# Query weights times keys made once instead of queries for every batch, one more tile weighed by GpSimd, and a new order

## The reference

```python
q = (x @ Wq).reshape(b, t, H, 2, DK)
q1, q2 = (q[..., 0, :], q[..., 1, :])
sim1 = jnp.einsum('bthd,hkd->bthk', q1, keys[:, :, 0, :])
sim2 = jnp.einsum('bthd,hkd->bthk', q2, keys[:, :, 1, :])
s1, i1 = jax.lax.top_k(sim1, K)
s2, i2 = jax.lax.top_k(sim2, K)
all_scores = (s1[..., :, None] + s2[..., None, :]).reshape(b, t, H, K * K)
all_indices = (i1[..., :, None] * NK + i2[..., None, :]).reshape(b, t, H, K * K)
final_scores, pk_idx = jax.lax.top_k(all_scores, K)
final_indices = jnp.take_along_axis(all_indices, pk_idx, axis=-1)
w_down = e_down[final_indices]
w_up = e_up[final_indices]
hidden = jnp.einsum('btd,bthkd->bthk', x, w_down)
hidden = jax.nn.silu(hidden)
hidden = hidden * jax.nn.relu(final_scores)
out = jnp.einsum('bthk,bthkd->btd', hidden, w_up)
```

## Time and profile before

| | us |
|---|---|
| median of three runs | 388.55 |
| profiled execution | 388.38 |
| its span, first to last instruction | 386.5 |

### The profile page before, as it was taken

One profiled execution on the slowest core, in us unless ns is written; L12 is line 12 of the kernel. 1 busy time (PEld: TensorE's weight loads), 2 busy tenths in 40 slices (PEclk: granted clock), 3 DMA queues, 4 the chain that ended last, 5 costly groups with the idle time before them and its releaser, 6 DMA issues.

```text
span 386.5 us, 8279 instructions
## 1 busy us (share of the span) xinstructions
PE 340.7 (88%) x3222; PEld 249.5 (65%) x3222; DVE 333.8 (86%) x838; ACT 246.8 (64%) x371; POOL 140.2 (36%) x194
## 2 busy tenths in 40 slices
PE   2898796688889889999969889998999999989997
PEld 2455453243334337688948767887888887778886
DVE  3989999999989997368877999999999999999940
ACT  3899999999998992237456687755766654011000
POOL 8737524612665644211001104255424148601000
PEclk9999999999989999999998999999999999999999
DMA  8940000000000008000000000000000000000000
GB/s 252 358 137 3 1 0 0 2 0 2 2 0 0 2 1 270 2 0 3 0 2 0 3 0 3 0 3 2 2 17 16 2 15 4 2 15 2 17 15 27
DMA packets 11142, 11.40 MB, mean 29 GB/s; under 512 B 608, under 2 KB 10592, under 8 KB 11104
## 3 DMA queue, kind: packets, MB, share of 16 engines
q1 hardware_dynamic: 11104, 10.88, 8.7%
HBM read 9.83 MB, written 1.05 MB: 28 GB/s over the span
## 4 chain that ended last, share of the span: by engine, by line
DVE 46%; PE 31%; ACT 11%; issue 7%; DMA 2%; POOL 1%; SPq 1%; DVEq 0%; ACTq 0%; POOLq 0%
PE pair L934 7%; DVE arena L1663 6%; PE pair L772 5%; DVE arena L1653 4%; PE pair L626 3%; DVE i L1982 3%; DVE arena L2042 3%; PE pair L898 3%; DVE s L1976 3%; ACT arena L1200 2%; ACT arena L1203 2%; DVE arena L2038 2%; DVE XN L1588 2%; DMA arena<-in_L_ffn_keys_dram 2%; PE pair L920 2%
## 5 line engine op out<-in xcount | busy, mean ns | idle before, releaser
L1663 DVE TENSOR_REDUCE arena<-arena 128x16 f32<-128x1024 f32 x64 | 66.5, 1075 | 2.5 <-POOL arena L365 1.7
L898 PE MATMUL pair<-arena,EDT 128*128 128x256 f32 x256 | 60.2, 383 | 0.0
L934 PE MATMUL pair<-EU,arena 128*128 128x256 f32 x256 | 58.4, 382 | 0.6 <-DVE arena L2066 0.6
L934 PEld LDWEIGHTS pair<-EU,arena 128*128 128x128 f32 x256 | 47.9, 190 | 7.4 <-issue 1.0
L898 PEld LDWEIGHTS pair<-arena,EDT 128*128 128x128 f32 x256 | 47.1, 190 | 6.5 <-ACT arena L1454 0.2
L644 PE MATMUL pair<-arena,WQ 128*128 128x512 fp8e4 x112 | 33.8, 383 | 15.8 <-ACT arena L1203 7.8
L488 POOL TENSOR_TENSOR arena<-arena 128x512 f32<-128x512 f32 x20 | 27.6, 1394 | 45.1 <-ACT arena L1446 45.1
L1200 ACT ACTIVATE arena<-pair,sq_bias 128x1024 f32<-128x1024 f32 x32 | 38.4, 1199 | 2.0 <-issue 1.5
L1186 ACT ACTIVATE arena<-arena,clip_bias 128x1024 fp8e4<-128x1024 f32 x32 | 39.5, 1235 | 0.0
L656 PE MATMUL pair<-arena 128*128 128x512 fp8e4 x128 | 38.6, 384 | 1.0 <-ACT arena L1186 1.0
L1454 ACT ACTIVATE arena<-pair 128x512 f32<-128x512 f32 x32 | 19.0, 598 | 27.2 <-PE pair L898 27.1
(11 more groups left out here) (201 smaller groups left out, 666.1 us busy)
## 6 DMA issues: line engine op xcount, KB each, us to landing
arena<-in_L_ffn_e_down_dram SPq DMA_DIRECT2D x1, 2048.0 KB, 12.5
EU<-in_L_ffn_e_up_dram SPq DMA_DIRECT2D x1, 2048.0 KB, 9.2
arena<-in_L_ffn_w_fc_dram SPq DMA_DIRECT2D x2, 512.0 KB, 5.4
X<-in_x_dram SPq DMA_DIRECT2D x1, 1024.0 KB, 6.2
arena<-in_L_ffn_w_proj_dram SPq DMA_DIRECT2D x1, 1024.0 KB, 13.7
GUW<-in_fside_BxS2xS_dram SPq DMA_DIRECT2D x1, 1024.0 KB, 11.4
out_dram<-arena SPq DMA_DIRECT2D x8, 128.0 KB, 1.7
CTX<-in_ctx_dram SPq DMA_DIRECT2D x1, 512.0 KB, 4.9
```

Source lines behind the costliest of these rows:

```text
L898: last = pe.matmul(bk2(4 + i % 2)[:, r, :], EDT[:, k, at:at + P], xT4[:, b % 2, k, :], start=(k == 0), stop=(k == 1))
L934: last = pe.matmul(bk2(7)[:, n, :], PR[:, n, e, :], EU[:, e, :], start=(e == 0), stop=(e == EROWS - 1))
L1663: dve.tensor_reduce(err[:, g // NS % 2, :, g % NS], squares, AX.X, ALU.add).then_inc(s["reduced"], 1)
```

## The change

1. No queries. The product of query weights and keys is made once: query_weights_transposed() transposes Wq by heads, key_weights(k) multiplies it by the keys, 256 features in two halves k, and ACT copies the result to WK. sims(b, n) multiplies the tokens by WK: four products of 128x512 over 128 rows, where it were eight of 128x128 over 64. WK takes the place of qT4, the transposed weights that of yo, eqs and sums.
2. Tile 5's coefficients are copied by ACT and weighed by POOL; DVE weighs tiles 6 and 7 only.
3. experts(b, ...) waits for the tokens and no longer for the queries' copies.
4. The lists of all engines from ffn1(8) on are in a new order: batch 1's integer layer stands beside batch 0's, ffn2 of batches 0 and 1 comes first, x3(1) and c_round(2) come before top8(0), and the ups and scatters are spread differently.

```diff
-        qT4 = cut(22 * KI, 2 * KI).rearrange("p (s h t) -> p s h t", s=2, h=H)
+        WK = cut(22 * KI, 2 * KI).rearrange("p (k a n) -> p k a n", k=2, a=2)
+        WQT = cut(24 * KI, KI).rearrange("p (h d) -> p h d", h=H)
-        DVE_WEIGHS = NT - 3
+        DVE_WEIGHS = NT - 2
...
-            def half_queries(b, lo, hi_):
-
-                pe.wait_ge(s["d_xT_e"], b + 1)
-                for i in range(lo, hi_):
-                    if b:
-                        pe.wait_ge(s["d_g_e"], 8 * b - 1 + i)
-                    for h in range(2):
-                        for k in range(2):
-                            c0 = (2 * i + h) * P
-                            last = pe.matmul(bk2(4 + i)[:, h, :], WQ1[:, k, c0:c0 + P], xT4[:, b % 2, k, :],
-                                             start=(k == 0), stop=(k == 1))
-                    last.then_inc(s["d_q_t"], 1)
+            def query_weights_transposed():
+
+                pe.wait_ge(ld["wq1"], 16)
+                pe.wait_ge(s["wT_e"], 8)
+                pe.wait_ge(s["guwT_e"], B)
+                for h in range(H):
+                    for k in range(2):
+                        last = pe.transpose(bk2(h // 2)[:, h % 2, k * P:k * P + P], WQ1[:, k, h * P:h * P + P],
+                                            ident[:, :])
+                last.then_inc(s["wqT_t"], 1)
+
+            def key_weights(k):
+
+                pe.wait_ge(s["wqT_e"], 2)
+                if k:
+                    pe.wait_ge(s["wk_e"], 2 * k)
+                for h in range(H):
+                    for a in range(2):
+                        rows = slice(a * DK, a * DK + DK)
+                        last = pe.matmul(bank[a][:, h * NK:h * NK + NK], WQT[rows, h, k * P:k * P + P],
+                                         keysT[rows, h, :], start=True, stop=True)
+                last.then_inc(s["wk_t"], 1)
 
             def sims(b, n):
                 t = 2 * b + n
                 if not t:
-                    pe.wait_ge(s["guwT_e"], B)
-                pe.wait_ge(s["d_q_e"], 2 * b + 2)
+                    pe.wait_ge(s["wk_e"], 4)
+                pe.wait_ge(s["d_xT_e"], b + 1)
                 if t:
                     pe.wait_ge(s["d_simread"], t)
-                for h in range(H):
-                    for a in range(2):
-                        last = pe.matmul(bank[a][:, h * NK:h * NK + NK],
-                                         qT4[a * DK:a * DK + DK, b % 2, h, n * P:n * P + P],
-                                         keysT[a * DK:a * DK + DK, h, :], start=True, stop=True)
+                for a in range(2):
+                    for k in range(2):
+                        last = pe.matmul(bank[a], xT4[:, b % 2, k, n * P:n * P + P], WK[:, k, a, :],
+                                         start=(k == 0), stop=(k == 1))
                 last.then_inc(s["d_sim_t"], 1)
 
             def experts(b, lo, hi_):
 
                 for i in range(lo, hi_):
                     g = 8 * b + i
-                    if i < 2:
-                        pe.wait_ge(s["d_q_e"], 2 * b + 1 + i)
+                    if i == 0:
+                        pe.wait_ge(s["d_xT_e"], b + 1)
+                    if g < 2:
+                        pe.wait_ge(s["x2"], g + 1)
                     else:
                         pe.wait_ge(s["d_g_e"], g - 1)
...
-            def queries(b, halves=(0, 1)):
-                for i in halves:
-                    act.wait_ge(s["d_q_t"], 2 * b + i + 1)
-                    act.copy(qT4[:, b % 2, 2 * i:2 * i + 2, :], bk2(4 + i)).then_inc(s["d_q_e"], 1)
+            def query_weights_out():
+
+                act.wait_ge(s["wqT_t"], 1)
+                for i in range(2):
+                    act.copy(WQT[:, 2 * i:2 * i + 2, :], bk2(i)).then_inc(s["wqT_e"], 1)
+
+            def key_weights_out(k):
+
+                act.wait_ge(s["wk_t"], k + 1)
+                for a in range(2):
+                    act.copy(WK[:, k, a, :], bank[a]).then_inc(s["wk_e"], 1)
 
...
-            weigh(5, (0, 1))
-            top8(7)
-            weigh(5, (2,))
             pair_top8(7)
-            weigh(5, (3,))
```

## The result

The changed kernel takes 389.46 us (median of 17 runs, 388.87 to 392.22), the kernel before 386.65 beside it on the same chip (17 runs, 385.08 to 388.98): ratio **1.0081, interval 1.0058 to 1.0105**. The change is a small loss: the time lies inside my range, and it moved the other way than I had forecast.

A forecast was written before the change was run, and what follows sets the result against it. No single bound: PE to 200.2 us, DVE and PE both nearly full from 212.1 to 341, then PE. 215.3 + 162.2 + 3.3 + 0.8 + 2.6 = 384.2, plus 0.7: span 384.9, time 386.8; range 381 to 392.5.

The forecast's parts named there:

- the price of sims: On PE: eight records of each wide sims take 3.44 us instead of 1.09, eight times, +18.8 us.
- the sum of the parts: PE's work: queries -13.8 us, sims +18.8, products made once +3.1, together +8.1 us.
- the waits: PE's waits: 3.4 us to ffn2's end, 2.7 to the first sims, 3.3 after, plus 0.7 for stretched DVE instructions.
- rival D: Shared ports, late scatters: four added GpSimd products each push one DVE instruction by 1.0 us; 387.8 us, no gain; chance 0.06.
- the order's first effect: x3(1) and c_round(2) done before top8(0), DVE 3.7 us ahead at the first sims; the stall before 343.13 goes.
- the work in the walk: PE's work from 145.9 us: 53.8 to ffn2's end, 9.5 to the first sims, 162.2 us from there on.
- The 0.8 us for the clock: PE's clock loss after gaps at 204 to 208 us: bounds 0 and 1.6, taken as 0.8 us.
- Rival A: The forecast: PE takes 8 us more work and gives back about as much in waits; within 1%, chance 0.43.
- DVE's lead: DVE 3.7 us ahead at the first sims, later eaten by waits; one_hots(0) to one_hots(5) end at 240.4 to 336.6 us.
- The baseline: The kernel before at 388.55 us, median of three runs; its profiled span was 386.5 us.
- B (waits fall out): PE's waits fall out entirely because DVE's lead is larger; 381.1 us, deciding from 384.7 down; chance 0.35.
- C (DVE waits for sims): sims gates top8, 3.44 us instead of 1.09 seven times; 392.1 us and over, deciding from 392.4 up; chance 0.16.

The follow-up runs named there:

- e13: The changed kernel with the casts of the indices (ranks) made by DVE right after its maxima instead of by GpSimd; 389.64 us, ratio 1.0053.
- e11: The changed kernel with twelve records in each sims instead of eight, 13.8 us more on PE; 404.74 us, ratio 1.0426.
- e5: The changed kernel with half the work in sims, four records instead of eight, 13.8 us less on PE; 386.42 us, ratio 0.9979.
- e10: The changed kernel with half the work in sims and a shortened last product of one_hots on DVE for tiles 1 to 7; 380.19 us, ratio 0.9774.
- e6: The changed kernel with three unforeseen waits (up(0, 0, 0, 4), c_clip(1), result(2)) moved out of PE's way; 387.84 us, ratio 1.0032.
- e12: e6 with a fourth wait covered: scatter(2, 0, 0) stands behind another quarter of up(1, 1); 388.99 us, ratio 1.0045.
- e2: The changed kernel with its new order and tile 5, but queries and narrow sims of before, no key_weights; 398.03 us, ratio 1.0282.
- e7: The changed kernel with the last seven squares of the hidden layer made by ScalarE instead of GpSimd; 391.32 us, ratio 1.0091.

## Why the prediction was wrong, point by point

**Right: the price of sims and the sum of the parts.** Eight records of sims took 3.43 us undisturbed (3.44 in the sum). PE's busy time in the four stages rose from 225.0 to 230.9 us, 6.0, and by 7.6 with the 1.6 of clock that before had in it: 8.1 in the sum.

**Right in the sum, and by luck: the waits.** The terms for them were 3.4, 2.7 and 3.3 + 0.7, 10.1 us. PE's idle time up to the last up was 59.1 - 55.9 = 3.2, 13.1 - 10.8 = 2.3 and 168.8 - 164.2 = 4.6, again 10.1 us. That the sum fits is luck, for the single waits were others: 1.05 at 183.09, 1.37 at 260.37 and 0.94 at 316.87 I did not have, and as much of those that I had was smaller or missing.
- 1.05 at 183.09 was for c_clip(1), which stood behind the two maxima of the gate weights on DVE. I had followed the operation, not the two that were put ahead of it.
- 1.37 at 260.37 was for the cast that DVE's one-hot products held. The row of this very effect stood in the earlier trace rows, 4.69 us at 251.68, and I had priced it only for the four *added* products in the tail (rival D), not for what the new list had put behind an *old* one.
- 0.94 at 316.87 was for result(2) behind look_up(4).

**Right: the order's first effect.** DVE had x3(1) and c_round(2) behind it when the first top8 began, at 218.12; the stall of the earlier trace rows at 343.13 is gone; PE's share of the time from 218 to the last up is 97% (164.3 us busy of 168.9).

**The step that failed: the work in the walk.** Its three terms, 53.8, 9.5 and 162.2, make 225.5 us of work for PE; measured were 55.9, 10.8 and 164.2, 230.9 us, 5.4 more. The 0.8 us for the clock was 0, as the granted clock of 1.00 shows. 5.4 - 0.8 = 4.6 is the whole difference between the span of 384.9 forecast and 389.5 found: 145.9 + 225.5 + 10.1 + 0.8 + 2.6 against 145.9 + 230.9 + 10.1 + 0 + 2.6.

The two halves of the prediction did not fit each other, and that could have been seen. Before had 225.0 us of PE work in these stages, 1.6 of it lost clock; with the 8.1 of the sum by parts that gives 231.5, almost what came. The walk had 225.5, 6.0 less, so that only 2.1 us of the 8.1 arrived in its end. With 231.5 in the walk and no clock loss the span would have been 390.1, above before's 386.5, and the forecast slower. Rival A's words, that the waits give back about as much as the 8 us, have no numbers behind them: my own terms took idle time from 15.6 to 12.7 us, 2.9 less, and that is what came.

Where the walk's work was too small, from start to start and without the waits: the small products (transpositions, factors, the integer layer, pre) took 27.5 us where I had 13.2 + 2.6 + 8.4 = 24.2, and the rest is spread over ffn1, ffn2, experts, up and sims. One reason shows in the rows: a group ahead of a wait runs to its full length, four transposes 0.66 instead of 0.44 us and eight records of experts 1.99 instead of 1.73, while my prices were from start to start in an unbroken list. With 15 waits in the list that would be some 3 us of the 5.4, an estimate from these two rows.

**DVE's lead was overstated.** The walk had one_hots(0) to one_hots(5) end at 240.4, 255.5, 279.5, 295.4, 315.8 and 336.6; they ended at 242.4, 257.7, 285.3, 301.6, 321.4 and 342.6. About two of the six are the late start, 3.6 more were lost between the second and the third. 2.35 of them are a wait of DVE at 266.10 for PE's c_x_transposed(3), which stands behind the late up(0, 0, 0, 4) and which the walk did not have.

**The baseline.** The walk was made on one execution; over its 17 runs before was 386.65, not 388.55. The profiled execution of the changed kernel was one of its longer ones too, 391.38, so that the spans compared above belong together. The baseline shifts both kernels and not their ratio, which I had 1.25% too low.

**The rivals.** A (forecast): the time of 389.46 is at the upper edge of A's own range, but PE's work was not given back: 7.6 us more of it against 2.9 of idle time and 1.6 of clock. B (waits fall out): no; 10.1 us of them remain. C (DVE waits for sims): DVE waited 3.3 us in three places for sims' line, under the 5 that I had set. D (ports): in the tail DVE's one-hot products at 352.40 and 355.70 took 3.37 and 2.83 beside the added GpSimd products, but scatter(3, 0) did not wait; in the middle, where nothing was added, PE lost 1.37. The Trainium skill (SBUF — State Buffer, section "SBUF: two separate sides") calls the shared pair of ports an exclusive lock for a whole instruction, which the engine has that starts first. The traces agree in the sum: in e13 two GpSimd products and two one-hot products took 6.2 us together, and alone they take 2.5 + 2.28 + 1.75 = 6.5. They differ in who has to wait: the cast's record starts 0.04 us ahead of DVE's, yet DVE's two instructions had their undisturbed length (2.28 and 1.75 us), and the cast was not let in between them either.

**What the loss is.** PE's work +7.6, its clock loss -1.6, and its idle time in the four stages, by the two tables, from 240.6 - 225.0 = 15.6 to 243.6 - 230.9 = 12.7, -2.9: +3.1, the difference of the spans (3.0). e11 says that more work costs its full price in this order. e5 says that taking off as much brings a third; the rest goes into waits (6.2 us) and lost clock (3.4), and e10 shows that with less work on DVE more of it comes back. What isn't settled is how much of the loss a better order could save: e6 shows 1.6 to 1.8 us, e12 that the next one is not to be had this way.

## What to carry to other kernels

Before you trust a walk, add up its work and hold it against the busy time that was measured before plus the change's own sum: here the two were 6.0 us apart, more than the whole effect, and the waits, on which the care had gone, came out right in the sum.

Where two engines are level, as here, work can have two prices: added, 13.8 us cost 13.7; removed, they brought 4.3. Measure both sides before a product is swapped for a larger one.

In a walk made ahead of the run, go through what stands *ahead* of the awaited instruction on its own engine, and look for a short GpSimd instruction beside long ones of DVE: here one of 0.24 us lasted 4.09, and all behind it came later. And an order is tuned to the lengths in it: here each half of the change cost 11 us of late part alone, as I had placed it, and both together 2.8.

## What the runs showed of the hardware that I had not expected

- A cast of 64 columns on GpSimd took 4.09 us (0.24 elsewhere) in the changed kernel, in e2 and in e5, each time until DVE's two one-hot products had ended, to 0.1 us.
- A gap on PE can cost twice. After 4.46 us (e5) and 4.63 us (e2) of waiting the granted clock was at 0.50 for some 3 and over 6 us; after two short gaps of 0.89 and 0.75 us in e12 a sims took 5.40 instead of 3.70. The changed kernel itself had gaps of 0.87, 0.23 and 0.90 us from 206 to 212 and kept 1.00. In e7 the same 0.87 and 0.23 us, from 208 to 210, were followed by a granted clock of 0.60 and 0.55 up to 214. So the length of a gap alone did not decide it.
